# Layer norm over channels: variances kept as rows, the inverse root spread by selection matmuls, and one layout written height-outside

## The reference

```
mu = mean(x, axis=1); var = var(x, axis=1)                # over the 16 channels
x1 = (x - mu) / sqrt(var + 1e-5) * ln_w + ln_b
out1, out2 = sums of depthwise convolutions of x1 along width / along height, then proj
... two attentions, per head: over rows (out3) and over columns (out4)
result = proj(out3) + proj(out4) + x
```

## Time and profile before

| | |
|---|---|
| median of 3 runs | 521.62 us (521.18 to 524.71) |
| the profiled execution, its own time | 524.1 us |
| its span, first to last instruction | 522.3 us |
| busy PE, DVE, ACT, POOL | 442.7, 389.4, 264.3, 44.3 us |
| granted clock of TensorE, mean | 0.922 of full |
| l0_norm | from the start to 44.75 us |
| l0_out | 187.3 to 220.0 us |

### The profile page before, as it was taken

One profiled execution on the slowest core, in us unless ns is written; L12 is line 12 of the kernel. 1 busy time (PEld: TensorE's weight loads), 2 busy tenths in 40 slices (PEclk: granted clock), 3 DMA queues, 4 the chain that ended last, 5 costly groups with the idle time before them and its releaser, 6 DMA issues. The chain is left out here.

```text
span 522.3 us, 18120 instructions
## 1 busy us (share of the span) xinstructions
PE 442.7 (85%) x7952; PEld 351.7 (67%) x7952; DVE 389.4 (75%) x597; ACT 264.3 (51%) x362; POOL 44.3 (8%) x64
## 2 busy tenths in 40 slices
PE   4588999994899919878999999849977899999971
PEld 2276999993799812255877778638745687777860
DVE  2795576987688895547899999847733889999963
ACT  0665432333333300038888888631105888888863
POOL 3320000000000000130000040000031000000000
PEclk9968999997799977969999999979996999999986
DMA  8830000000000000000000000000000000000004
GB/s 187 196 137 1 1 3 3 3 3 0 3 3 2 1 1 0 1 0 3 4 4 3 0 0 4 4 2 0 1 0 1 3 4 3 3 0 1 4 3 161
DMA packets 8093, 9.79 MB, mean 19 GB/s; under 512 B 5440, under 2 KB 6752, under 8 KB 7904
## 3 DMA queue, kind: packets, MB, share of 16 engines
q1 hardware_dynamic: 7008, 8.60, 5.8%
q10 hardware_dynamic: 1024, 0.28, 0.3%
HBM read 6.76 MB, written 2.11 MB: 17 GB/s over the span
## 5 line engine op out<-in xcount | busy, mean ns | idle before, releaser
L1068 DVE TENSOR_TENSOR g_wgt<-g_exponents,ps 128x1024 f32<-128x1024 f32 x128 | 151.0, 1205 | 5.0 <-PE ps L913 4.8
L1012 ACT ACTIVATE g_wgt<-g_wgt 128x1024 f32<-128x1024 f32 x128 | 132.4, 1061 | 18.7 <-DVE g_wgt L1068 17.9
L913 PE MATMUL ps<-ident,g_scl 128*128 128x128 f32 x512 | 80.3, 287 | 3.8 <-DVE g_scl L1059 3.6
L928 PEld LDWEIGHTS ps<-g_wgt,g_xt 128*32 128x32 f32 x4096 | 61.1, 111 | 21.7 <-issue 18.6
L928 PE MATMUL ps<-g_wgt,g_xt 128*32 128x64 f32 x4096 | 71.1, 222 | 2.7 <-issue 2.6
L913 PEld LDWEIGHTS ps<-ident,g_scl 128*128 128x128 f32 x512 | 57.3, 140 | 15.3 <-DVE g_scl L1059 4.9
L996 ACT ACTIVATE g_hid<-ps,vec 128x512 f32<-128x512 f32 x32 | 22.0, 688 | 66.0 <-PE ps L872 66.0
L450 PE MATMUL ps<-projblk,conv_img 128*64 128x64 f32 x1024 | 53.3, 266 | 0.7 <-DVE xcol L500 0.6
L450 PEld LDWEIGHTS ps<-projblk,conv_img 128*64 128x64 f32 x1024 | 52.7, 194 | 1.2 <-DVE xcol L500 1.1
L1309 PE MATMUL ps<-high,wb 128*128 128x512 f32 x72 | 30.2, 420 | 5.3 <-DVE rest L1338 5.3
L1309 PE MATMUL ps<-rest,wb 128*128 128x512 f32 x72 | 30.0, 417 | 0.0
(11 more groups left out here) (156 smaller groups left out, 671.0 us busy)
## 6 DMA issues: line engine op xcount, KB each, us to landing
x<-in_x SPq DMA_DIRECT2D x8, 256.0 KB, 6.6
x<-in_x SPq DMA_DIRECT2D x1, 2048.0 KB, 8.6
out<-g_result SPq DMA_DIRECT2D x4, 512.0 KB, 3.9
windows<-band SPq DMA_DIRECT2D x4, 256.0 KB, 5.0
c_weight<-in_c_weight SPq DMA_DIRECT2D x1, 576.0 KB, 4.2
g_w<-in_g_w SPq DMA_DIRECT2D x2, 128.0 KB, 2.6
g_gband<-in_g_gband SPq DMA_DIRECT2D x2, 64.0 KB, 2.7
centre<-in_centre SPq DMA_DIRECT2D x1, 64.0 KB, 2.3
```

The costliest lines, as they stand in the source:

```text
L913: tr = pe.transpose(ps[:, u % 4, P * k:P * k + P], spread(scl[s][:, k, u:u + 1], [P, P]), ident[:])
L928: mm = pe.matmul(ps[32 * j:32 * j + 32, O_BANK, 64 * cb:64 * cb + 64], xt[(s + t) % 2][:, cb, b, :], wgt[s][b][:, t, cb, :], start=(t == 0 ...
L1012: act.activation(w, w, ACT.Exp).then_inc(weight, 1)
L1068: dve.tensor_tensor(wgt[s][u][:], spread(gband[:].unsqueeze(2), shape), spread(s_in, shape), ALU.mult).then_inc(logit, 1)
```

## The change

Chunks are cut into 16 pieces of 256 pixels. Sixteen matmuls with four variants of `meansel` add up in one bank: partition 32q + 8c + b holds the variance of batch b in piece 4q + c. These rows are rooted straight out of PSUM, with epsilon as the bias, and inverted, both in two halves of 128 columns. Thirty-two matmuls with 0/1 matrices `planesel`, each reading 32 partitions (a row tile), copy each row to the partitions of its batch in the eight banks. Turning, gathering and `widen` are gone. Chunks are then treated in the order 0, 2, 4, 6, 1, 3, 5, 7. The constants on ACT's DMA queue get semaphores of their own; `meansel` grows from 128x32 to 128x128 values, and `planesel` with 128x512 values is new. In l0_out the column transposes are written with height outside and width inside.

```diff
@@ build: the two views of the dead row and column layouts
-                               [t[:].rearrange("p n b h -> p (n b h)").rearrange("p (q a l) -> p q a l", q=2, l=32)
-                                for t in (xrow, xcol)])
+                               [t[:].rearrange("p n b h -> p (n b h)").rearrange("p (q a l) -> p q a l", q=2, l=l)
+                                for t, l in ((xrow, W), (xcol, W // 2))])
@@ l0_norm: tiles
-    meansel = sb("meansel", [P, 32])
-    var_row = sb("var_row", [P, 2 * BANK])
+    meansel = sb("meansel", [P, 4, 32])
+    planesel = sb("planesel", [P, 4, P])
+    PIECE = PIX // 16
-    wide = sb("wide", [P, PXT, CP, B, HEADS])
+    VAR_BANK, BIAS_BANK = 7, 6
+    ORDER = (0, 2, 4, 6, 1, 3, 5, 7)
@@ l0_norm: TensorE
+            def average(q):
+                for c in range(4):
+                    piece = 4 * q + c
+                    if c % 2 == 0:
+                        pe.wait_ge(squared, piece // 2 + 1)
+                    mm = pe.matmul(ps[32 * q:32 * q + 32, VAR_BANK, 0:PIECE], meansel[:, c, :],
+                                   sq[:, PIECE * piece:PIECE * piece + PIECE], start=(c == 0), stop=(c == 3))
+                if q == 3:
+                    mm.then_inc(var_mm, 1)
+            pe.wait_ge(meansel_in, 16)
+            pe.wait_ge(xc_copied, 8)
+            for q in range(3):
+                average(q)
             pe.wait_ge(const_in, 16 * CONSTS)
...
+            average(3)
-            for a in range(2):
-                pe.wait_ge(xc_copied, 6 + a)
-                for q in range(4):
-                    pe.wait_ge(squared, 4 * a + q + 1)
-                    mm = pe.matmul(ps[32 * q:32 * q + 32, 5 + a, :], meansel[:],
-                                   sq[:, BANK * (4 * a + q):BANK * (4 * a + q + 1)], start=True, stop=True)
...
+            for h in range(2):
+                pe.wait_ge(rstd_ready, h + 1)
                 for c in range(4):
-                    tr = pe.transpose(ps[:, a, P * c:P * c + P], var_row[:, BANK * a + P * c:BANK * a + P * c + P],
-                                      ident[:])
+                    if h == 0 and c == 2:
+                        pe.wait_ge(rooted, 2)
+                    for q in range(4):
+                        rows = slice(32 * q, 32 * q + 32)
+                        at = slice(h * PIECE // 2, (h + 1) * PIECE // 2)
+                        mm = pe.matmul(ps[:, 2 * q + c // 2, :].rearrange("p (s f) -> p s f", s=2)[:, c % 2, at],
+                                       planesel[rows, c, :], rstd[rows, at], start=True, stop=True)
+                    if h == 1 and c % 2 == 1:
+                        mm.then_inc(rstd_spread, 1)
@@ l0_norm: ScalarE
+            act.dma_start(meansel[:], d["meansel"]).then_inc(meansel_in, 16)
+            act.dma_start(planesel[:], d["planesel"]).then_inc(planesel_in, 16)
-            act.wait_ge(const_in, 16 * CONSTS)
...
-            act.wait_ge(var_mm, 2)
-            act.copy(var_row[:, BANK:2 * BANK], ps[:, 6, :]).then_inc(var_out[1], 1)
-            act.wait_ge(eps_added, 2)
-            act.activation(std[:], var[:], ACT.Sqrt).then_inc(rooted, 1)
-            act.wait_ge(rstd_ready, 1)
-            for j in range(CHUNKS):
-                widen(act.copy, j, 1)
+            act.wait_ge(eps_set, 1)
+            act.wait_ge(var_mm, 1)
+            for h in range(2):
+                part = slice(h * PIECE // 2, (h + 1) * PIECE // 2)
+                act.activation(std[:, part], ps[:, VAR_BANK, part], ACT.Sqrt, bias=eps[:, 0:1], scale=1.0).then_inc(rooted, 1)
@@ l0_norm: VectorE
-            dve.tensor_copy(var_row[:, 0:BANK], ps[:, 5, :]).then_inc(var_out[0], 1)
...
-                dve.tensor_scalar(var[:].rearrange("p (a q c b) -> p a q c b", a=2, q=4, c=4)[:, a], tiles,
-                                  LN_EPS, None, ALU.add).then_inc(eps_added, 1)
...
-            dve.reciprocal(rstd[:].rearrange("p t b -> p (t b)"), std[:]).then_inc(rstd_ready, 1)
-            for j in range(CHUNKS):
-                widen(dve.tensor_copy, j, 0)
+            for h in range(2):
+                part = slice(h * PIECE // 2, (h + 1) * PIECE // 2)
+                dve.wait_ge(rooted, h + 1)
+                dve.reciprocal(rstd[:, part], std[:, part]).then_inc(rstd_ready, 1)
+            for k, j in enumerate(ORDER):
+                dve.wait_ge(rstd_spread, k // 4 + 1)
@@ l0_out
-                          turned_c[:, q, left:left + HALF_W, first:first + STRIP].rearrange("p w h -> p h w"),
+                          turned_c[:, q, first:first + STRIP, left:left + HALF_W],
-                dve.transpose(turned_c[:, q, part], columns[:, q, part]).then_inc(cols_turned, 1)
+                dve.transpose(turned_c[:, q, :, part].rearrange("p h w -> p w h"), columns[:, q, part])
@@ shape_constants
-    meansel = ((plane_b[:, None] == np.arange(32)) / C).astype(np.float32)
+    row_c, row_b = np.divmod(np.arange(32), B)
+    meansel = ((plane_b[:, None, None] == row_b) & (row_c == np.arange(4)[:, None])).astype(np.float32) / C
+    planesel = np.tile((meansel.transpose(2, 1, 0) > 0).astype(np.float32), (4, 1, 1))
```

More of the change, by code:

```diff
@@ L158, in l0_norm @@
     sq = sb("sq", [P, PIX])
-    var = sb("var", [P, PXT * B])
-    std = sb("std", [P, PXT * B])
-    rstd = sb("rstd", [P, PXT, B])
-    wide = sb("wide", [P, PXT, CP, B, HEADS])
+    std = sb("std", [P, PIECE])
+    rstd = sb("rstd", [P, PIECE])
     x_in = [sem(f"x_in{j}") for j in range(4)]
@@ L177, in l0_norm @@
     var_mm = sem("var_mm")
-    var_out = [sem(f"var_out{a}") for a in range(2)]
-    var_turned = sem("var_turned")
-    eps_added = sem("eps_added")
+    eps_set = sem("eps_set")
     rooted = sem("rooted")
     rstd_ready = sem("rstd_ready")
-    rstd_wide = [sem(f"rstd_wide{cp}") for cp in range(CP)]
     rstd_spread = sem("rstd_spread")
@@ L189, in l0_norm @@
     evac_s = sem("evac_s")
-    CONSTS = 8
+    CONSTS = 6
+    meansel_in = sem("meansel_in")
+    planesel_in = sem("planesel_in")
+    ident_in = sem("ident_in")
+    VAR_BANK, BIAS_BANK = 7, 6
+    ORDER = (0, 2, 4, 6, 1, 3, 5, 7)
     with nc.Block() as block:
@@ L241, in _ @@
+            pe.wait_ge(meansel_in, 16)
+            pe.wait_ge(xc_copied, 8)
+            for q in range(3):
+                average(q)
             pe.wait_ge(const_in, 16 * CONSTS)
-            pe.wait_ge(xc_copied, 5)
             for t in range(2):
-                mm = pe.matmul(ps[:, 4, C * t:C * t + C], spread(bias_lhs[:, t:t + 1], [nb, P]),
+                mm = pe.matmul(ps[:, BIAS_BANK, C * t:C * t + C], spread(bias_lhs[:, t:t + 1], [nb, P]),
                                bias_rhs[:], start=True, stop=True)
@@ L265, in _ @@
[L265 to L273, removed]
+            average(3)
+            pe.wait_ge(planesel_in, 16)
@@ L275, in _ @@
+            pe.wait_ge(ident_in, 16)
             for base, lines in ((0, sq[:].rearrange("p (i m) -> p i m", m=P)),
                                 (CHUNKS, sq[:].rearrange("p (m i) -> p i m", m=P))):
-                for g in range(CHUNKS):
+                for k, g in enumerate(ORDER):
                     if base == 0:
-                        pe.wait_ge(normed, g + 1)
+                        pe.wait_ge(normed, k + 1)
                     else:
-                        pe.wait_ge(evac_s if g % 2 else evac_v, g // 2 + 1)
+                        pe.wait_ge(evac_s if k % 2 else evac_v, k // 2 + 1)
@@ L291, in turned_in @@
             return ps[:, g, :].rearrange("p (i m) -> p i m", m=P)
[L293 to L297, removed]
         @block.scalar
@@ L323, in _ @@
             for lay, base in ((xrow, 0), (xcol, CHUNKS)):
-                for g in range(1, CHUNKS, 2):
-                    act.wait_ge(turned, base + g + 1)
-                    act.copy(turned_out(lay, g), turned_in(g)).then_inc(evac_s, 1)
+                for k in range(1, CHUNKS, 2):
+                    act.wait_ge(turned, base + k + 1)
+                    act.copy(turned_out(lay, ORDER[k]), turned_in(ORDER[k])).then_inc(evac_s, 1)
         @block.vector
         def _(dve):
+            dve.memset(eps[:], LN_EPS).then_inc(eps_set, 1)
             dve.wait_ge(taps_in, 16)
@@ L361, in _ @@
             for lay, base in ((xrow, 0), (xcol, CHUNKS)):
-                for g in range(0, CHUNKS, 2):
-                    dve.wait_ge(turned, base + g + 1)
-                    dve.tensor_copy(turned_out(lay, g), turned_in(g)).then_inc(evac_v, 1)
+                for k in range(0, CHUNKS, 2):
+                    dve.wait_ge(turned, base + k + 1)
+                    dve.tensor_copy(turned_out(lay, ORDER[k]), turned_in(ORDER[k])).then_inc(evac_v, 1)
 def l0_conv(nc, sem, sb, ident, pair, ps, xrow, xcol, toep, projblk, beta, o1c, o2r, rn):
@@ L770, in on_vector @@
                 part = slice(STRIP * j, STRIP * j + STRIP)
-                dve.transpose(turned_c[:, q, part], columns[:, q, part]).then_inc(cols_turned, 1)
```

(4 more changed lines are left out.)

29 lines of the change are left out of this document (10 added, 19 removed).

## The result

The change is faster, by less than forecast: 517.88 us (median of 16, 515.68 to 521.11) against 523.18 (median of 16); ratio 0.9914, 95% interval 0.9893 to 0.9934, so 4.5 us. The time lies in the stated range; the forecast was 7.15 us and "faster by over 1%", and 0.9% is short of that. Of the 3.4 us by which 517.88 misses 514.5, 1.6 is the starting point: 16 runs of before have the median 523.18, the three of the table 521.62. The profiled execution was the quickest of the sixteen (515.68, span 513.0), 8.4 us under that of before: two single executions say too much here, and the stages have to be read one by one.

The account below looks back on a forecast made before the run. No engine is always busy and stages follow a meeting of all engines, so gains count per stage. Layer norm 1.75 + PE in l0_out 5.7 − transposes 0.3 = 7.15 us, from 521.6 to 514.5; range 511.0 to 519.5.

Parts of the forecast that it names:

- Step and low clock: l0_out, PE: adjacent reads bring L745 from 1.79 to 0.87 us, only 0.1 won at lower clock; 5.7 us in all.
- The 0.3 us for the transposes: l0_out, DVE: eight column transposes writing with a step cost 0.04 us more each, 0.3 us on the path.
- C: Rival, l0_out: the stride is paid twice in a transpose, 7.4 us more in front of PE, 521.6 us; chance 0.10.
- E: Rival, l0_out: stepped output leaves the transposer line by line, next block waits; 15 us more, 529 us; chance 0.04.
- F: Rival, l0_out: L745 is slow for another reason than its step and stays so; 520.2 us; chance 0.05.
- Serial column tiles: Layer norm, variances: matmuls in turn share 32 array columns and can't run side by side; ACT released at 24.15 us.
- exposed table load: Layer norm, root: the 1.28 us table load carries the wait for the variances and so falls on the path.
- DMA term: Layer norm: 304 KB of constants on ACT's queue delay x by 0.7 us, bounds 0 and 1.27.
- the chain from the last copy to the first multiplication: Layer norm: last centred copy ends at 17.33 us, DVE's first multiplication comes at 28.55 instead of 30.30.
- B: Rival, layer norm spreading: row tiles run one after the other, 3.5 us lost, 518.0 us; chance 0.12.
- D: Rival, layer norm: inverse halves wait for POOL, first multiplication 3.9 us later, 518.5 us; chance 0.07.
- the old widening's stalls beside POOL: Layer norm before: two of DVE's eight widening copies stand beside POOL's operations; 7.7 us of widening on the path goes.

Follow-up runs that it names:

- ln_mended: The changed kernel with variance matmuls c outside and q inside, the variance wait ahead of epsilon's, and planesel on SP's queue behind x; ratio 0.9828.
- out_pe_shift: The kernel before with only the new l0_out column layout, plus 70 idle PE instructions in the pause ahead of L745; ratio 0.9937.
- pool_late: The kernel before with one wait holding POOL's Toeplitz products back until DVE's eight widening copies are done; ratio 0.9897.
- out_only: The kernel before with only the three l0_out edits (column block written height outside); ratio 0.987, 6.8 us faster.
- ln_only: The changed kernel with the old l0_out layout, so the new layer norm alone; ratio 1.0109, 5.7 us slower than the kernel before.
- change_pe_shift: The changed kernel with 186 idle PE instructions ahead of the first L735, so later ones lie 256 places behind the kernel before; ratio 0.9981.

## Why the prediction was right, and where it was not

- *l0_out, 5.4 forecast, 5.7 to 5.9 in three traces.* Step and low clock as said. The 0.3 us for the transposes did not come (7.45 against 7.47), so the stage gave about the 5.7 of PE alone. Rivals C, E and F did not happen.
- *Layer norm, 1.75 forecast, 3.0 to -0.4 in six traces, 1.3 on average.* Serial column tiles and the exposed table load were right in place and size (6.0 and 1.28), and ln_mended shows them by their removal. The DMA term was too small: 0.7 with bounds of 0 and 1.27 taken, 1.5 on average measured and up to 2.5, which the prediction had named as a sign of being wrong. The clock in the spreading, 1.3 us in three of six, stood only in the range. Against these, the chain from the last copy to the first multiplication was 0.5 shorter than the sum has it (10.72 against 11.22), and ACT's eight copies took 7.15 us where it kept 7.65; the old order of chunks shows 7.26 and 7.19 (out_pe_shift, pool_late) and 7.61 (out_only), so whether the order does that is open. B and D did not happen.
- *The sum, 7.15, against 4.5.* The stages gave 1.3 and 5.8, so 7.1, which is the forecast. What the prediction had wrong is that all after l0_out is merely moved. It counted PE's new records by their time alone, but the 70 more instructions of the program put gaps of 1.0 and 1.4 us into the ends of the blurs and cost 3.5 us in the medians (out_pe_shift against out_only; 4.8 in the traces). The gaps are 2.3 of the 4.8. Of the rest it is known that out_pe_shift has the lower clock from 495.5 to 498.9 us, ahead of the second gap, where out_only has not; why is not shown. The other way, the first blur of the change starts at the full clock and that of before doesn't, some 3 us by the traces; how many executions of before do so was not measured. So 7.1, less 3.5 to 4.8, plus 0 to 3, gives 2 to 7 us, an estimate from these traces; the 4.5 lies inside, and it can't be split more finely. These two terms of opposite sign were both left out, and that the time fell into the range owes something to luck: ln_only, the same layer norm without l0_out, is 5.7 us slower than before.
- The account of the old widening's stalls beside POOL was right, but its use was not seen: holding POOL back gives as much as the change.

## What to carry to other kernels

Before rebuilding a slow piece, look for the few instructions that are slow in it (8 copies, six at 281 ns and two at ten times that) and what runs beside them. Put neighbouring small matmuls in different tiles of the array, and see which of several waits a table load carries. A change of PE's program by 70 instructions can move the time by as much as the change itself, so compare the untouched stages too, and read a stage from several traces before its gain is believed.

## What the runs showed of the hardware

A gap of 0.9 to 1.4 us with no wait, inside a run of matmuls, came with 70 idle PE instructions far ahead (out_pe_shift) and went with 186 more (change_pe_shift); a 16 KB transfer of instructions ended within 0.4 us of its start. Such an idle instruction took about 0.1 us (186 in 19.7 us). DVE's copy out of and into SBUF took up to 3.7 us instead of 0.28 beside POOL's product, while its reciprocals of 128 columns (0.92 us each, against 0.95 in the earlier trace rows) and its products with PSUM (0.61 each) were not held. Selection matmuls of 128 columns whose neighbours differ in the row tile took 32 ns a record, with neighbours in the same one 75, at the full clock. A DVE transpose of 128x512 took 0.58 us with adjacent elements on both sides and 0.85 to 0.93 with a step on one or both.
